# Three places for the transposed count groups in the first pooling, and one output buffer for the feature sums

## The reference

```
row, col = src, dst                                  # first network
pooled = segment_sum(h[col], row, num_segments=6250) # and again in its second layer
pooled = pooled * inv_deg
x = relu(batchnorm(pooled @ W0 + b0)); x = x @ W1 + b1; h = relu(batchnorm(x))
...
messages = concat(nodes[src], edge_attr_32) @ W_message.T      # third network
aggregated = segment_sum(messages, dst, num_segments=6250)
```

## Time and profile before

| | us |
|---|---|
| runs of the kernel before | 3440.25, 3454.41, 3460.50 |
| their median | 3454.41 |
| the profiled execution | 3444.14 |
| its span | 3442.0 |

### The profile page before, as it was taken

One profiled execution on the slowest core, in us unless ns is written; L12 is line 12 of the kernel. 1 busy time (PEld: TensorE's weight loads), 2 busy tenths in 40 slices (PEclk: granted clock), 3 DMA queues, 4 the chain that ended last, 5 costly groups with the idle time before them and its releaser, 6 DMA issues. The chain is left out here.

```text
span 3442.0 us, 42796 instructions
## 1 busy us (share of the span) xinstructions
PE 3108.4 (90%) x18237; PEld 1780.0 (52%) x18237; DVE 902.6 (26%) x1697; ACT 733.4 (21%) x1172; POOL 158.3 (5%) x119
## 2 busy tenths in 40 slices
PE   1799789995999689999999999997999768999998
PEld 1688644552444245555555555553555664555554
DVE  6999712223100430100001010004100562111111
ACT  4799611114000410000000000001000472000000
POOL 5000033330000000000000000000000000000000
PEclk6899889997999899999999999999999878999999
DMA  7244699973566045555555555551655102555554
GB/s 245 76 132 132 164 192 155 176 129 79 134 152 143 0 137 140 137 143 142 141 141 141 140 138 144 148 146 47 174 151 152 36 38 79 141 141 142 144 141 134
DMA packets 740822, 453.39 MB, mean 132 GB/s; under 512 B 349204, under 2 KB 736302, under 8 KB 740048
## 3 DMA queue, kind: packets, MB, share of 16 engines
q1 hardware_dynamic: 706290, 412.62, 48.3%
q10 hardware_dynamic: 32702, 31.44, 3.0%
q0 software_dynamic: 1664, 6.92, 0.6%
HBM read 316.30 MB, written 54.34 MB: 108 GB/s over the span
## 5 line engine op out<-in xcount | busy, mean ns | idle before, releaser
L1967 PE MATMUL acc<-tbuf,hs 128*128 128x448 fp8e4 x8232 | 1573.6, 353 | 1.9 <-PEq L1172 1.9
L1967 PEld LDWEIGHTS acc<-tbuf,hs 128*128 128x128 f16 x8232 | 805.7, 98 | 765.0 <-issue 30.1
L1545 PE MATMUL acc<-tbuf,hs 128*128 128x512 fp8e4 (+1 forms) x1300 | 285.7, 373 | 21.7 <-DMA tbuf<-table 21.7
L703 PE MATMUL quad<-K,S 128*128 128x196 bf16 x1568 | 277.0, 249 | 16.0 <-DVE K L643 11.8
L683 ACT ACTIVATE stage<-quad 128x784 fp8e4<-128x784 f32 x392 | 289.4, 828 | 8.8 <-PE quad L703 5.3
L707 PE MATMUL deg<-K,S 128*128 128x196 bf16 x1568 | 275.8, 247 | 0.0
L1427 PE MATMUL acc<-tbuf,hs 128*128 128x512 fp8e4 (+1 forms) x1300 | 266.4, 368 | 0.7 <-issue 0.7
L1275 PE MATMUL acc<-tbuf,hs 128*128 128x448 fp8e4 x1372 | 259.7, 352 | 2.9 <-DVEq L1310 2.9
L2094 DVE SCALAR_TENSOR_TENSOR B<-acc,scales,C 128x448 f32<-128x448 f32 x56 | 38.1, 681 | 805.3 <-PE acc L1967 805.3
L2073 ACT ACTIVATE H<-B,vectors 128x448 f32<-128x448 f32 x56 | 37.4, 668 | 876.6 <-DVE B L2098 876.6
L1275 PEld LDWEIGHTS acc<-tbuf,hs 128*128 128x128 f16 x1372 | 133.7, 98 | 128.7 <-issue 4.6
(11 more groups left out here) (282 smaller groups left out, 1899.4 us busy)
## 6 DMA issues: line engine op xcount, KB each, us to landing
tbuf<-table SPq DMA_DIRECT2D x343, 448.0 KB, 3.5
tbuf<-table SPq DMA_DIRECT2D x343, 336.0 KB, 3.1
table<-stage SPq DMA_DIRECT2D x6, 5488.0 KB, 19.5
feat<-in_edge_attr_dram ACTq DMA_DIRECT2D x27, 448.0 KB, 5.6
C<-factors ACTq DMA_DIRECT2D x2, 3136.0 KB, 11.8
table<-stage SPq DMA_DIRECT2D x2, 2744.0 KB, 12.2
A<-x_kept ACTq DMA_DIRECT2D x1, 3136.0 KB, 10.3
C<-factors SPq DMA_DIRECT2D x1, 3136.0 KB, 11.1
```

What stands on the lines that cost most here:

```text
L703: mm = T.matmul(pair[quad % 3][:, at:at + NKEY], S[:, q, i, :], K[:, q, i, :], start=(w % 2 == 0), stop=True, skip_group_check=True)
L1545: mm = T.matmul(acc[g % 2][:, 0:n * P], k.hs[:, j, part, :], counts[:, :, j // 2, :, j % 2], start=(j == 0 and part == 0), stop=(j == NL - ...
L1967: mm = nc.tensor.matmul(acc[h][:, 0:HALF], rows[:, g * US + r, part, :], counts[:, (r - lo) * STRIP + h * HALF:(r - lo) * STRIP + (h + 1) ...
```

## The change

`table_buffer` takes the number of groups that have a place, 2 as a default; the first pooling asks for 3 (`AHEAD`). There group g lies in place g % 3 with semaphores `table_in0` to `table_in11`, SP issues the reads of groups 1 and 2 at once and those of group g, from 3 on, after group g-3 has been used. The tensors `sums_e` and `zeros_e` are gone: the sums have one buffer, and the zeros a block, both in `k.raw`. The copy of half h now waits for the write of half h-1. The clearing matmul reads 224 columns of zeros twice. SP no longer counts turns there.

```
-def table_buffer(k, over_src=False):
+def table_buffer(k, over_src=False, groups=2):
-    ... TSIZE], F16)
+    ... groups * 4 * TU], F16)

-def turned_done(k):
-    for h in range(2):
+def turned_done(k, groups=2):
+    for h in range(groups):
         for b in range(4):
-            ... for g in range(h, NSG, 2) if b < width(g)])
+            ... for g in range(h, NSG, groups) if b < width(g)])

+AHEAD = 3
 def pool_with_features(k, dst, tbuf, ea):
-        sums = sb("sums_e", [NEA, 2, HALF], F32)
-        zeros = sb("zeros_e", [P, HALF], BF16)
+        free = k.raw[:, :, :].rearrange("p a b -> p (a b)")
+        sums, zeros = free[0:NEA, 0:HALF], free[:, HALF:].bitcast(BF16)
-        a_in = [k.sem(f"table_in{b}") for b in range(NSLOT)]
+        a_in = [k.sem(f"table_in{b}") for b in range(4 * AHEAD)]
                 for g in range(1, NSG):
-                    if g >= 2:
-                        sp.wait_ge(used.h, used.at(g - 1))
-                        sp.sem_inc(turn.h, 1)
-                    load_turned(k, sp, tbuf, g, g % 2, width(g))
+                    if g >= AHEAD:
+                        sp.wait_ge(used.h, used.at(g - AHEAD + 1))
+                    load_turned(k, sp, tbuf, g, g % AHEAD, width(g))
                 def clear(b):
-                    T.matmul(eab[b][0:NEA, 0:HALF], zeros[:, 0:NEA], zeros[:, :], start=True, stop=True)
+                    T.matmul(eab[b][0:NEA, 0:HALF].rearrange("p (a f) -> p a f", a=2), zeros[:, 0:NEA],
+                             zeros[:, 0:HALF // 2].unsqueeze(1).to_broadcast([P, 2, HALF // 2]), start=True, stop=True)
-                        slot = g % 2 * 4 + b
-                        pe.wait_ge(a_in[slot].h, a_in[slot].at(g // 2 * 16 + 16))
-                    counts = turned_view(tbuf, g % 2, n)
+                        slot = g % AHEAD * 4 + b
+                        pe.wait_ge(a_in[slot].h, a_in[slot].at(g // AHEAD * 16 + 16))
+                    counts = turned_view(tbuf, g % AHEAD, n)
-                V.memset(zeros[:, :], 0.0).then_inc(ea_set.h, 1)
+                V.memset(free[:, HALF:], 0.0).then_inc(ea_set.h, 1)
                 def read(h, b, n=HALF):
                     act.wait_ge(z_used.h, z_used.at(min(h + 1, NHALF) * HZB))
-                    if h >= 2:
-                        act.wait_ge(sums_out[b].h, sums_out[b].at(h // 2 * 16))
-                    A.activation(sums[:, b, 0:n], eab[b][0:NEA, 0:n], ACT.Copy).then_inc(ea_read.h, 1)
+                    if h:
+                        act.wait_ge(sums_out[1 - b].h, sums_out[1 - b].at((h + 1) // 2 * 16))
+                    A.activation(sums[:, 0:n], eab[b][0:NEA, 0:n], ACT.Copy).then_inc(ea_read.h, 1)
                     act.wait_ge(ea_read.h, ea_read.at(h + 1))
-                    act.dma_start(..., sums[:, b, 0:n]).then_inc(sums_out[b].h, 16)
+                    act.dma_start(..., sums[:, 0:n]).then_inc(sums_out[b].h, 16)
-    turned_done(k)
+    turned_done(k, AHEAD)

-        with table_buffer(k) as tbuf:
+        with table_buffer(k, groups=AHEAD) as tbuf:
             prepare(k, tbuf)
             pool_with_features(k, k.B, tbuf, w["edge_attr_32"])
```

More of the change, by code:

```diff
@@ L1102 @@
 TSIZE = NSLOT * TU
-def table_buffer(k, over_src=False):
-    return k.nc.sbuf_tensor(f"tbuf{k.next()}", [P, NBUF * 4 * SU if over_src else TSIZE], F16)
+def table_buffer(k, over_src=False, groups=2):
+    return k.nc.sbuf_tensor(f"tbuf{k.next()}", [P, NBUF * 4 * SU if over_src else groups * 4 * TU], F16)
 def load_piece(k, sp, tbuf, s, i):
@@ L1137, in turned_view @@
         "p (b j l t) -> p b j l t", b=4, l=P, t=2)[:, 0:n]
-def turned_done(k):
-    for h in range(2):
+def turned_done(k, groups=2):
+    for h in range(groups):
         for b in range(4):
-            k.sem(f"table_in{h * 4 + b}").base += 16 * len([g for g in range(h, NSG, 2) if b < width(g)])
+            k.sem(f"table_in{h * 4 + b}").base += 16 * len([g for g in range(h, NSG, groups) if b < width(g)])
 def split_and_pool(k, v, at, dst, factor, weight=None, own=None, load_factor=True, layer=None, keep=False):
@@ L1475, in pool_with_features @@
         eas = sb("eas", [P, 2, PIECE * 4, NEA], BF16)
-        sums = sb("sums_e", [NEA, 2, HALF], F32)
-        zeros = sb("zeros_e", [P, HALF], BF16)
+        free = k.raw[:, :, :].rearrange("p a b -> p (a b)")
+        sums, zeros = free[0:NEA, 0:HALF], free[:, HALF:].bitcast(BF16)
         acc = [k.bank[h] for h in range(2)]
         eab = [k.bank[2], k.bank[3]]
-        a_in = [k.sem(f"table_in{b}") for b in range(NSLOT)]
-        used, acc_read, turn = k.sem("turned_used"), k.sem("src_read"), k.sem("turn_pool")
+        a_in = [k.sem(f"table_in{b}") for b in range(4 * AHEAD)]
+        used, acc_read = k.sem("turned_used"), k.sem("src_read")
         ea_in, ea_set = [k.sem("ea_in0"), k.sem("ea_in1")], k.sem("ea_set")
@@ L1622, in read @@
                     act.wait_ge(z_used.h, z_used.at(min(h + 1, NHALF) * HZB))
-                    if h >= 2:
-                        act.wait_ge(sums_out[b].h, sums_out[b].at(h // 2 * 16))
-                    A.activation(sums[:, b, 0:n], eab[b][0:NEA, 0:n], ACT.Copy).then_inc(ea_read.h, 1)
+                    if h:
+                        act.wait_ge(sums_out[1 - b].h, sums_out[1 - b].at((h + 1) // 2 * 16))
+                    A.activation(sums[:, 0:n], eab[b][0:NEA, 0:n], ACT.Copy).then_inc(ea_read.h, 1)
                     act.wait_ge(ea_read.h, ea_read.at(h + 1))
-                    act.dma_start(k.ea_sums[:, h * HALF:h * HALF + n], sums[:, b, 0:n]).then_inc(sums_out[b].h, 16)
+                    act.dma_start(k.ea_sums[:, h * HALF:h * HALF + n], sums[:, 0:n]).then_inc(sums_out[b].h, 16)
                 load(0)
```

## The result

| | before | after |
|---|---|---|
| median of the runs, us | 3447.07 (11 runs) | 3431.59 (11 runs) |
| profiled execution's span, us | 3442.0 | 3427.5 |

The ratio of after to before is 0.9951, 95% interval [0.994, 0.9962]: 0.49% less; the medians lie 15.5 us apart. The forecast was 15 us less, and 3439 us as a time, counted from a median of 3454.4 us of three runs. Over eleven runs the kernel before has a median 7 us lower, and so the time came out 7 us under the forecast.

A forecast was written before the change was run, and what follows sets the result against it. TensorE, busy 90% of the span, loses time where it waits, here for table reads. Waits and clocks -16.9 us, stage's end +2.0, sum -14.9, say -15: from 3454.4 to 3439 us, range 3424 to 3457.

The forecast's parts named there:

- The waits: TensorE at starts of groups in the first pooling: five waits for table reads, 12.9 us, go; with clocks 16.9 us.
- The stage's end: Last copy of the sums must wait for the write before it to land: 2.0 us added, bounds 1.2 and 8.
- The one buffer in mid-stage: Copy of each half waits for the previous half's write, issued 22.2 us before the copy: cost 0.
- The pace: Reads of the first pooling: 22.6 to 24.9 us a group against TensorE's 25.8, DMA faster by 0.9 to 3.2.
- The first rival: DMA is the bound, the third place only spends a head start of 15 us: saving 5, 3449 us; chance 0.13.
- Head start: Group 2's reads follow at 459.8, not 475; group 3 is in at about 521, wanted at 526.9; no wait left.
- The rival of the single buffer: Writes slowed by reads delay ACT's copies, so TensorE waits for features in each of 13 halves: 3472 us; chance 0.05.

## Why the prediction was right, and which step was not

- The waits: right. All five went, and with two of them the stretches at the lower clock, 17.7 us between the ends of group 0 and group 12, forecast 16.9.
- The stage's end: right in kind, +1.3 us against 2.0. The landing of the write reached ACT faster than the 1.0 us that I allowed: the write is issued at 763.37 and the copy starts at 772.37, 9.0 us later, which is 7.7 of writing and 0.75 to its first byte and leaves some 0.6.
- The one buffer in mid-stage at no cost: right, ACT waits for a write once, at the end.
- "The pace": wrong. I forecast reads at 22.6 to 24.9 us a group and a lead that grows by 0.9 us; they take 27.0 and the lead shrinks by 1.2. The 22.6 was what is left when SP's waits are taken out of the stage. But feature loads and writes went on in those pauses, and cost the reads nothing there: of the first twelve writes of before, two go out with hardly a read beside them (551.7 and 739.2), of the change none. The 24.9 came from a stretch almost without pauses, but one with less beside the reads: ACT's queue moved 2.18 MB in its 49.7 us, 1.09 a group (and 0.73 in the stretch of 23.1 us), against 1.33 a group in the change (12.01 MB over nine groups). The first rival had the mechanism right (the third place spends a head start). Its threshold was 27 us a group over groups 2 to 11; they took 25.9, since nine of them took 27.0 and group 2, at the start, 15.8. That the forecast of the waits held although its pace was wrong is owed to the head start and to the shortness of the stage, and in that much it is luck: the reads were 10.7 us later at group 10 than I had them (694.6 against 683.9) and still 12 us early.
- "Head start": it was named for group 3 but given no price of its own, and the run without it shows it to be 7 to 9 of the 15.5 us.
- The rival of the single buffer did not happen: no write took more than 9.04 us from its first packet to its last, and 22 were needed.
- The cause of the slow reads was not looked for; I put it to sharing in general ("There the reads share the engines with the feature loads and the sums' writes"). The slow writes are what used up the DMA time: with them split, two places have no wait left and the change is worth nothing. The 7.7 us for 174 KB stood in the earlier trace rows, at 15 to 26 GB/s where the reads run at 290, and was used only as the length of a write.

## What to carry to other kernels

More places hide a late transfer only as far as they give a lead. The pace of a queue must be read from a stretch in which it runs without a pause and with all the traffic beside it that an average stretch has, not from the whole less the pauses. Before adding a buffer, look at the rates in slices for stretches in which all engines are busy and little moves: here a transfer of 97 rows made them, and splitting it was worth more (24 us, each beside its own runs of before) than 25.6 KB of SBUF in each partition (15.5). Of a double buffer that is given up, look at the last two uses, where nothing stands between them.

## What was not expected of the hardware

- A write of 174 KB in 97 rows takes 7 to 9 us on one engine. Where the transposing reads go beside it, all that moves falls from 290 to about 70 GB/s. As 96 rows and 1 row it takes 0.5 to 1.8 us and leaves no such stretch.
- A second set of 14 such writes costs 91 us, 6.5 us for each in the mean.
- A load of 3136 KB issued beside the reads of a group made that group 17.9 us late, though C is needed only at a group's end.
